# A delta rule whose last sixteen decay factors are made among the projection's columns

## What is computed

```python
qkv = x @ w_qkv                      # 64 column blocks of 128: 16 q, 16 k, 32 v
z = x @ w_z                          # 32 column blocks: the output gate
beta = sigmoid(x @ w_b)
g = -exp(a_log) * softplus(x @ w_a + dt_bias)
q, k, v = split(silu(causal_conv(qkv)))           # 4 taps
q = l2norm(q) * 128 ** -0.5 ; k = l2norm(k)
g = cumsum(g)                        # along the 64 tokens
decay = where(lower, exp(g_i - g_j), 0)
A = where(strict, -(beta * k @ k.T) * decay, 0)
attn = solve_triangular(eye - A, eye)
v_c = attn @ (beta * v)
o = where(lower, q @ k.T * decay, 0) @ v_c        # state is zero
out = (rmsnorm(o) * norm_w * silu(z)) @ w_out
```

## Time and profile before

| | before |
|---|---|
| median of 3 runs | 2787.28 us (2786.14 to 2788.21) |
| the profiled execution | 2785.56 us, of which its span is 2783.8 |
| PE busy | 2640.7 us (95%) |
| DVE, ACT, POOL busy | 1864.2, 1574.8, 505.4 us |
| granted PE clock | 0.983 of full |
| the columns of the delta rule | 1870.9 to 2187.1 us of the span |
| its tail | 2198.8 to 2371 us |

### The profile page before, as it was taken

One profiled execution on the slowest core, in us unless ns is written; L12 is line 12 of the kernel. 1 busy time (PEld: TensorE's weight loads), 2 busy tenths in 40 slices (PEclk: granted clock), 3 DMA queues, 4 the chain that ended last, 5 costly groups with the idle time before them and its releaser, 6 DMA issues.

```text
span 2783.8 us, 39649 instructions
## 1 busy us (share of the span) xinstructions
PE 2640.7 (95%) x13810; PEld 2190.6 (79%) x13810; DVE 1864.2 (67%) x4737; ACT 1574.8 (57%) x2992; POOL 505.4 (18%) x428
## 2 busy tenths in 40 slices
PE   6889999999999999999999999999998778998999
PEld 5778788887887887887887887878876668777887
DVE  7747648548547557557466477668668776668997
ACT  7945536436436446345445355436676567857776
POOL 4402002002002012011011020015353332022111
PEclk9989999999999999999999999999999899999999
DMA  3432013022022031031130121435676542549996
GB/s 125 136 122 85 12 53 94 15 68 75 18 78 61 20 91 43 24 94 30 28 99 15 40 85 48 152 120 161 178 214 183 128 93 68 185 187 360 378 371 228
DMA packets 255062, 317.92 MB, mean 114 GB/s; under 512 B 128712, under 2 KB 166216, under 8 KB 241808
## 3 DMA queue, kind: packets, MB, share of 16 engines
q1 hardware_dynamic: 251392, 310.03, 35.5%
q0 software_dynamic: 3040, 5.08, 0.7%
q10 hardware_dynamic: 432, 0.27, 0.0%
HBM read 274.22 MB, written 46.98 MB: 115 GB/s over the span
## 4 chain that ended last, share of the span: by engine, by line
PE 79%; DVE 10%; ACT 4%; issue 2%; DMA 2%; POOL 1%; SPq 1%; POOLq 0%; DVEq 0%; ACTq 0%
PE ps L103 21%; PE ps L105 21%; PE ps L104 21%; PE ps L874 3%; PE ps L830 3%; PE ps L902 2%; DVE lnw L2159 2%; DVE zz L2162 1%; PE ps L895 1%; PE ps L855 1%; PE ps L1344 1%; PE ps L1343 1%; PE ps L2000 1%; DVE cv L2126 1%; PE ps L579 1%
## 5 line engine op out<-in xcount | busy, mean ns | idle before, releaser
L1244 POOL TENSOR_TENSOR lnw<-lnw,half 128x8 f32<-128x8 f32 x88 | 144.4, 1641 | 1217.6 <-DVE lnw L964 1217.6
L103 PE MATMUL ps<-whf,cth 128*128 128x512 f32 (+1 forms) x832 | 336.5, 405 | 1.8 <-ACT kn L1117 1.8
L103 PE MATMUL ps<-cnh,pth 128*128 128x512 f32 (+1 forms) x832 | 330.0, 397 | 6.5 <-issue 4.6
L105 PE MATMUL ps<-whf,ctl 128*128 128x512 f32 (+1 forms) x832 | 326.3, 392 | 0.0
L104 PE MATMUL ps<-wlf,cth 128*128 128x512 f32 (+1 forms) x832 | 325.5, 391 | 0.0
L104 PE MATMUL ps<-cnl,pth 128*128 128x512 f32 (+1 forms) x832 | 324.9, 390 | 0.0
L105 PE MATMUL ps<-cnh,ptl 128*128 128x512 f32 (+1 forms) x832 | 324.6, 390 | 0.0
L2652 DVE TENSOR_TENSOR ml<-mr,mh 128x2048 fp32r<-128x2048 f32 x90 | 203.3, 2286 | 26.8 <-ACT mh L2594 26.8
L1155 ACT ACTIVATE pr<-ps,sm 128x1601 f32<-128x1601 f32 x56 | 89.6, 1600 | 204.8 <-DVE sm L1017 204.8
L1180 ACT ACTIVATE xo<-ps 128x128 f32<-128x128 f32 x64 | 17.7, 277 | 312.8 <-PE ps L902 312.8
L1036 DVE TENSOR_TENSOR ptl<-ps,pth 128x512 fp32r<-128x512 f32 (+1 forms) x256 | 139.1, 585 | 78.8 <-ACT pth L1167 78.4
(11 more groups left out here) (349 smaller groups left out, 6413.1 us busy)
## 6 DMA issues: line engine op xcount, KB each, us to landing
mr<-in_moe SPq DMA_DIRECT2D x90, 1024.0 KB, 7.1
ctr<-in_ctxt SPq DMA_DIRECT2D x96, 256.0 KB, 3.0
pr<-in_ctxn SPq DMA_DIRECT2D x96, 256.0 KB
wv<-in_wv SPq DMA_DIRECT2D x64, 256.0 KB, 2.8
wr<-in_wqkv SPq DMA_DIRECT2D x64, 256.0 KB, 3.0
wvf<-in_wattn SPq DMA_DIRECT2D x11, 1024.0 KB, 4.9
ca<-cat_d SPq DMA_DIRECT2D x16, 512.0 KB, 3.9
qk_d<-cv SPq DMA_DIRECT2D x32, 256.0 KB, 3.3
```

What stands on the lines that cost most here:

```text
L103: pe.matmul(dst, lh, rh, start=first, stop=False)
L105: return pe.matmul(dst, ll, rh, start=False, stop=last)
L1244: po.tensor_tensor(rs[0:w, s, :], nv[0:w, s, :], half[0:w, 0:8], ALU.pow).then_inc(kx_rs, 1)
```

## The change

- The factors of groups 16 to 31 are made ahead, in the columns' part. In four bursts from position 44, nine positions apart, `factor_load` loads for 16 heads of one tile (four groups) the gates and beta from `gb_d` and now also the turned query norms from `rq_d`, in 256-byte pieces; POOL adds mask and column term (`pg_mask`, two instructions in each of two positions), ACT takes the exponential of 1024 elements (`pg_exp`), POOL multiplies beta with it and then it with the query norms (`pg_scale`, again two instructions in each of two positions), and `factor_store` stores 1 MB to `cf_d`. The tiles `pg` and `pgr` lie where `mt` and `xt` come to lie, so that these are cleared at position 80 (`clear`) and not at 38.
- In the tail `gate_load` fetches rows of 4 KB from `cf_d`, POOL and ACT have no part in builds 16 to 31, and DVE's `second` makes the coupling with two instructions of half the size. `p3` for n >= 16 is a plain copy with factor 1 by DVE. The outputs for n < 16 alternate between ACT (even) and DVE (odd).
- Value columns come earlier: at four places (k = 6, 12, 18, 24) two stand in succession, so that the last is at position 91, and positions 92 to 95 are gate columns. There the solve's budget is 2000 a position.
- At `norm2` a third transpose, of `rq`, with its copy and store.

```diff
@@ places and order
+        GATE_PLACES, VALUE_PLACES, place = [], [], 32
+        for k in range(32):
+            if k not in (6, 12, 18, 24):
+                GATE_PLACES.append(place)
+                place += 1
+            VALUE_PLACES.append(place)
+            place += 1
+        GATE_PLACES += list(range(place, NPOS))
@@ building(n)
                 yield "build", n, 0
-                yield "decay", n, 0
@@ stage_order, among the columns
+                burst, r = divmod(s - 44, 9)
+                if 0 <= burst < 4:
+                    if r == 0:
+                        yield "pg_load", burst, 0
+                    if r in (2, 3):
+                        yield "pg_mask", burst, r - 2
+                    if r == 4:
+                        yield "pg_exp", burst, 0
+                    if r in (5, 6):
+                        yield "pg_scale", burst, r - 5
+                    if r == 7:
+                        yield "pg_store", burst, 0
+                if s == 80:
+                    yield "clear", 0, 0
...
-                    yield from some(steps, 700)
+                    yield from some(steps, 700 if s < 92 else 2000)
@@ SP
+            if m >= 8:
+                sp.wait_ge(*d_cf.at(16 * ((m - 8) // 2 + 1)))
...
+                if m >= 8:
+                    sp.dma_start(dst.rearrange("p f h a t -> p (f h a t)"),
+                                 cf_d[(m - 8) // 2, 64 * b:64 * b + 64, 1024 * (m % 2):1024 * (m % 2) + 1024]).then_inc(d_gb[m % 4].sem, 16)
...
+        def factor_load(sp, k):
+            sp.wait_ge(d_gt, 32)
+            if k > 0:
+                sp.wait_ge(*d_cf.at(16 * k))
+            for b in range(2):
+                sp.dma_start(pg[64 * b:64 * b + 64, :, :, :],
+                             gb_d[64 + 16 * k:80 + 16 * k, :, 64 * b:64 * b + 64].unsqueeze(0).to_broadcast([64, 16, 2, 64])).then_inc(d_pg.sem, 16)
+                sp.dma_start(pgr[64 * b:64 * b + 64, :, :],
+                             rq_d[64 + 16 * k:80 + 16 * k, 64 * b:64 * b + 64].unsqueeze(0).to_broadcast([64, 16, 64])).then_inc(d_pg.sem, 16)
+        def factor_store(sp, k):
+            sp.wait_ge(*pg_scaled.at(4 * k + 4))
+            sp.dma_start(cf_d[k], pg[:, :, :, :].rearrange("p h a t -> p (h a t)")).then_inc(d_cf.sem, 16)
@@ ACT
+                elif step == "pg_exp":
+                    ac.wait_ge(*pg_masked.at(8 * n + 8))
+                    ac.activation(pg[:, :, 0, :], pg[:, :, 0, :], ACT.Exp).then_inc(pg_exp.sem, 1)
...
-                elif step == "p3" and n < OUT_AC:
+                elif step == "p3" and on_ac(n):
@@ POOL
-                elif step == "start":
-                    po.wait_ge(d_gt, 16)
+                elif step == "pg_mask":
+                    e = pg[:, 8 * k:8 * k + 8, 0, :]
+                    po.wait_ge(*d_pg.at(64 * (n + 1)))
+                    po.tensor_tensor(e, e, negm.unsqueeze(1).to_broadcast([128, 8, 64]), ALU.add).then_inc(pg_masked.sem, 2)
...
+                elif step == "pg_scale":
+                    e, b, r = pg[:, 8 * k:8 * k + 8, 0, :], pg[:, 8 * k:8 * k + 8, 1, :], pgr[:, 8 * k:8 * k + 8, :]
+                    po.wait_ge(*pg_exp.at(n + 1))
+                    po.tensor_tensor(b, b, e, ALU.mult).then_inc(pg_scaled.sem, 1)
+                    po.tensor_tensor(e, e, r, ALU.mult).then_inc(pg_scaled.sem, 1)
+                elif step == "clear":
+                    po.wait_ge(*d_cf.at(64))
                     po.memset(mt[:, :, :, :], 0.0).then_inc(zeroed.sem, 1)
                     po.memset(xt[:, :, :, :], 0.0).then_inc(zeroed.sem, 1)
...
-                elif step == "build":
+                elif step == "build" and n < 16:
@@ DVE
+                    else:
+                        dv.wait_ge(*aq_out.at(n + 1))
+                        kk, over = (kqs[:, n % 4, :].rearrange("p (k a t) -> p k a t", k=2, a=2)[:, :, a, :] for a in range(2))
+                        t = vs(dv.tensor_tensor(over, pair(b)[:, :, 1, :], kk, ALU.mult))
+                        dv.wait_ge(dv_step, t)
+                        dv.tensor_tensor(kk, pair(b)[:, :, 0, :], kk, ALU.mult).then_inc(at_out.sem, 1)
...
-                elif step == "p3" and n >= OUT_AC:
+                elif step == "p3" and not on_ac(n):
...
+                    if n < 16:
+                        dv.tensor_tensor(vb[:, j, h:h + 4, :], src, rq[:, j, h:h + 4].unsqueeze(2).to_broadcast([128, 4, 128]),
+                                         ALU.mult).then_inc(apD_dv.sem, 1)
+                    else:
+                        dv.tensor_scalar(vb[:, j, h:h + 4, :], src, 1.0, None, ALU.mult).then_inc(apD_dv.sem, 1)
```

More of the change, by code:

```diff
@@ L1480, in program @@
         ssq = sb5g("ssq", [128, 32, 4])
-        gT = sb5g("gT", [128, 2, 128])
+        gT = sb5g("gT", [128, 3, 128])
         s5g.close()
+        s5p = ExitStack()
+        sb5p = stack_sb(s5p)
+        pg = sb5p("pg", [128, 16, 2, 64])
+        pgr = sb5p("pgr", [128, 16, 64])
+        s5p.close()
         mt = sb5("mt", [128, 2, 8, 128])
@@ L1514, in program, with on_ac, group_out @@
         rms_in, rms_out = Again(self_s, 8), Again(self_sub, 8)
-        OUT_AC = 20
-        NPOS = 96
+        d_pg, d_cf, pg_masked = Again(d_xo[1], 512), Again(cn_high, 104), Again(cn_low, 104)
+        pg_exp, pg_scaled, apD_dv = Again(ct_low, 104), Again(ct_high, 104), Again(wk_low, 4)
+        def on_ac(n):
+            return n < 16 and n % 2 == 0
+        def group_out(n):
+            return (apD_out if on_ac(n) else apD_dv).at(len([k for k in range(n + 1) if on_ac(k) == on_ac(n)]))
+        NPOS = 96
+        GATE_PLACES, VALUE_PLACES, place = [], [], 32
[6 more added lines that the diff above has]
+        GATE_PLACES += list(range(place, NPOS))
         def conv_of(s):
-            return s if s < 32 else None if s % 2 == 0 else 32 + (s - 32) // 2
+            return s if s < 32 else 32 + VALUE_PLACES.index(s) if s in VALUE_PLACES else None
         def gate_of(s):
-            return (s - 32) // 2 if s >= 32 and s % 2 == 0 else None
+            return GATE_PLACES.index(s) if s in GATE_PLACES else None
         def qkv_bank(s):
@@ L1774, in s5_sp @@
                     gz_store(sp, gate_of(i - 1))
+                elif step == "back":
+                    gz_store(sp, gate_of(NPOS - 1))
                 elif step == "turn" and i < 32:
@@ L1788, in s5_sp @@
                         gate_load(sp, q)
+                elif step == "pg_load":
+                    factor_load(sp, i)
+                elif step == "pg_store":
+                    factor_store(sp, i)
                 elif step == "load" and 10 <= i < 16:
@@ L1869, in s5_ac @@
                     ac.activation(gT[:, 0, :], bank(5)[:, 0:128], ACT.Copy, scale=-1.0)
-                    ac.activation(gT[:, 1, :], bank(5)[:, 128:256], ACT.Copy).then_inc(gT_out, 1)
+                    ac.activation(gT[:, 1:3, :].rearrange("p a t -> p (a t)"), bank(5)[:, 128:384], ACT.Copy).then_inc(gT_out, 1)
                 elif step == "evict":
@@ L2266, in s7_pe @@
                     if k == 0:
[L2267 removed]
+                        pe.wait_ge(*group_out(31))
                     if i == 0:
```

49 lines of the change are left out of this document (30 added, 19 removed).

## The result

The changed kernel takes 2815.95 us (median of 5 runs, 2811.35 to 2817.89). The kernel before, beside it, took 2786.84 (2785.99 to 2788.21). The ratio is 1.0104, with a 95% interval of 1.0093 to 1.0114. I had forecast 2778.4 and a range up to 2800, so the sign was wrong and the time lies above the range.

What follows compares the result with a forecast made beforehand. The prediction took PE to wait on DVE late in the weights part and in the tail; -9.1 - 0.5 - 15.3 + 16 = -8.9 us gave a forecast of 2778.4 us, range 2764 to 2800.

Steps and rivals of the forecast that it cites:

- The end of the weights: From the last column's matmuls to the tail's first: only one turn left, 2.6 us instead of 11.7, so -9.1 us.
- The -0.5 for the budgets: Positions 92 to 95, solve budget 2000 instead of 700: 1.5 us of split lateness goes, the last split comes 1 us late.
- The tail: The stretch behind the weights, in parts A to E, 172.2 us before: -15.3 us in sum.
- S: Start of the tail, its first matmuls, at 2198.84 us in the profile of the kernel before.
- A: Tail from S to the first step of solve 2, 51.05 us before: -18.0, with solve 2 starting at S + 33.
- B: Tail, solve 2, 39.0 us before: 37.7 with its steps, adds, `seconds` and three outputs, so -1.3 us.
- D: Tail, solve 3, 26.2 us before: six outputs at 0.683 us come onto DVE, so +4.0 us.
- E: Tail's store, fetch and last eight groups at PE's pace, 43.0 us before: no change, because PE is full there.
- step 1: Weights part, SP and POOL held by factor loads and masks: 2 to 3 us a burst, +5 for the two before 2075.
- step 2: Weights part, DVE from 2075 to 2151: +1.5 for an extra value column less a gate split, +9.5 for contention with POOL.
- the rival with the lock in full: POOL stops DVE for the whole of each instruction: contention 19.9 us instead of 9.5, time 2788.8; chance 0.15.
- the factor bursts stop the columns: Weights part: 6144 pieces hold SP, column loads and splits come late, 9 us a burst, 36 in all, 2799.9; chance 0.15.

Runs made afterwards that it cites:

- the loads are small and the masks in their old places: Changed kernel with 8 KB rows, three later bursts loading one head of 16, masks two positions behind: 2801.85 us; with POOL's instructions on 8 elements too, 2781.31.
- the places alone: Kernel before with only the new value and gate column places and the solve budget of 2000: 2776.24 us, ratio 0.9968; second series 2778.92.
- without the budgets: Kernel before with the new column places, but the solve budget at positions 92 to 95 kept at 700: 2776.72 us, ratio 0.9966.
- late masks and small instructions: Changed kernel, 8 KB rows, masks five and six positions behind the loads, POOL's instructions on 8 elements: 2781.34 us with full loads, 2773.61 with small.
- late masks: Changed kernel, bursts every 11 positions, masks five and six behind the loads: 2802.73 us; with 8 KB rows 2798.29; with one-head loads too 2788.16.
- the run with ACT's queue: Changed kernel with 8 KB rows, masks two positions behind, each burst's four factor loads issued by ACT instead of SP: 2802.27 us, ratio 1.0054.
- long rows: Changed kernel with the gates stored in two halves, so factor loads read 8 KB and 4 KB rows instead of 256-byte pieces: 2808.57 us, ratio 1.0082.

## Why the prediction was wrong

**The end of the weights: right**, -9.1 as forecast; one turn behind the last column. The -0.5 for the budgets had the wrong sign: at the last column they cost 3.0 us of waiting and about 2 us at half clock, which the tail gave back.

**The tail: right in sum**, -14.2 against -15.3, by parts that were off. The halved products are what I took them for: 0.29 us each, 0.85 for the pair for aq. `second` 23 ended at S + 25.2, not 22.7, because its instructions waited now and then for ACT and PE. From there to solve 2 it was 14.4 us and not 10.3. SP issued a load of qk, a pair of factor loads and four xt loads before it came to the coupling's loads at S + 30.3. These held it for 6.75 us, with the first solve step another 2.5 behind. In before the same four loads held it for 2.39 us (the third row); why it is more now, with the DMA engines 0.94 busy in part A against 0.64, is not tested:

```profile
2265.56 2.41 SPq L1796 DMA_DIRECT2D xt<-z_d  x4
2268.14 6.75 SPq L1867 DMA_DIRECT2D cv<-at_d  x4
...
2245.20 2.39 SPq L1805 DMA_DIRECT2D cv<-at_d  x4
```

So solve 2 started at S + 39.6 (33 was forecast), and A gave 11.5 instead of 18. B gave 3.4 instead of 1.3: counted from start to start, its 31 steps took 21.9 us where I had 22.3 and its six `seconds` 8.5 where I had 9.3, and five adds fell into it and not six. D was +1.9 instead of +4.0: five outputs fell into it and not six, and one add less than before; E -1.4.

**The weights part, step 1: this is the step that failed.** It gave SP and POOL 2 to 3 us for each of the first two bursts, and nothing for the later two. Measured are 7.5, 8.4, some 17 and some 11, in which step 2 and the places have their share. Four things in it were wrong.
- *The wait.* Loads were to land 11 us behind the issue and POOL to wait 5; in the first burst they landed at 12.7 and it waited 8.1, and 13.2 in the worst. I had scaled from pairs of 0.5 MB, whose 5.2 us come from a stretch with the DMA engines 0.79 busy; the 1.5 MB took 1.7 us more than that scaling in the first burst, and 3.7 in the third.
- *The lead.* Two positions were to be 6 us between the issue and POOL's arrival at the mask. They are places in the order and not times: SP's own weight loads wait for splits (51.4 us for POOL's and 42.2 for DVE's in the list of after), so SP issues late. POOL stood at the mask 4.7, 3.2, 3.0 and -0.2 us behind the first issue of its burst. In the first burst PE wanted its split at 2030.9, 14.5 us behind the issue; the landing, four instructions of the masks and the split end at 2035.7. PE waited 4.91 us where I had 1.3.
- *The clock.* I had nothing for what follows a wait. It is some 13 us over all columns, 67 matmuls at 0.63 us.
- *"In the later two DVE is later than they."* That was a guess without a row. These two bursts cost the most. A load that stops ACT's splits stops the evictions behind them, and DVE's convolutions wait for those: 43.9 us in after against 19.7 in the same list of before. DVE, already the limit, lost that too.

**Step 2: right in kind, too small.** I took 0.48 us of DVE for each us of POOL, and 19.9 us of POOL for two bursts. The factor was 0.58 to 0.80, and it holds in all four bursts, 37.7 us. It costs columns only where DVE is late, or where the loads no longer hide it: 8 us in after, 19 where the loads are small and the masks in their old places (351.8 against 333.2). That the 8 us lie near the 9.5 of the forecast is luck, since I had counted two bursts and not four, and no loads that hide the rest. By the factor, 0.80 is nearer to the rival with the lock in full (1.0), 0.58 nearer to my 0.48.

**The value columns: +1.5 forecast**; the places alone cost 6.5 (3.1 without the budgets). Most of it is the clock: 27 matmuls at 0.63 us, 5 us, against 2 in before, and 11 without the budgets.

**The rival that came true** is "the factor bursts stop the columns", with the right mechanism, SP, POOL and ACT in order behind 6144 pieces, and the wrong part of it in the lead: not the pieces but the bytes' landing. It had 9 us a burst; it should have had 10 to 11, and 6.5 instead of 1.5 for the places, which makes the 48.3. Its chance of 0.15 rested on the two columns of lead that spoke against it. The range's upper end took its price as the worst. The sign that I had named for it was there: PE stood 19.6 us at five of POOL's splits, 8.7 in the longest.

What stays open: with late masks and small instructions, full loads still cost 11 us (335.5 against 324.8). That they do is shown, and where: ACT waits 31.0 us for the weights of value columns with the full loads and 12.3 with the small ones, six times each. Whether these weights are late by the busy DMA engines or by their order behind the factor loads is not settled, since the run with ACT's queue had its masks in the old places.

## What to carry to other kernels

Work that is moved into a stage where the limiting engine "has slack" has to be priced on every engine and queue that issues, waits for and shares a port with it, in order: here a fifth to a third of idle DMA time and a half-idle GpSimd had no room for 6 MB of loads and 38 us. A load's consumer on an in-order engine must stand further behind the issue than the load takes to land at that place in the queue, or everything behind it pays; and the distance has to be read in us from both queues, not in positions of the order. A wait of the matmul engine costs more than itself where the clock falls behind it. Two costs that overlap each look small when one is cut alone; cut both before you call either harmless. And of a change with several parts, the part that only moved positions was worth having: alone it gave 0.2 to 0.3%.

## What the runs showed of the hardware

- DVE and POOL took turns, one instruction each: 0.80 us of DVE lost for each us added on POOL with the masks two positions behind the loads (the runs with small loads), 0.58 with late masks. DVE's convolutions, with one input from PSUM, kept 0.73 us.
- 6144 pieces of 256 bytes held SP 7.7 to 9.3 us in after, against 2.4 to 2.6 with long rows, but the 1.5 MB landed after 12.6 to 14.7 us and 11.6 to 14.5.
- After 3 us without work the matmuls ran at 0.63 us instead of 0.39 for seven in a row at the last column in after, and for eleven with the places alone. Over the columns of after 67 did, in eight rows behind waits of 1.8 to 8.7 us.
